# One pipeline over the eight retention and feed-forward units of a hybrid transformer kernel, with its first normalizations in one pass

## What is computed

```python
x = x + retention_net(layernorm(x))    # 2 layers
x = x + experts(layernorm(x))          # 8 experts, top 2 of the router
x = x + causal_attention(layernorm(x)) # 16 heads of 8 channels
x = x + experts(layernorm(x))          # same weights
# retention_net, for each layer:
p = layer_norm(x) @ proj_w + proj_b ; q, k, v, xo = split(p)
ret = ((q @ k.T) * D[head]) @ v        # D: decaying lower triangle, 16 heads
x = x + (ret * silu(xo)) @ reto_w + reto_b
h = layer_norm(x)
x = x + gelu(h @ ffn1_w + ffn1_b) @ ffn2_w + ffn2_b    # 128 -> 512 -> 128
```

## Time and profile before

| | |
|---|---|
| median of 3 runs | 881.59 us (880.51 to 881.97) |
| the profiled execution | 881.72 us |
| its span, first to last instruction | 879.9 us |
| busy: TensorE, DVE, ScalarE, GpSimd | 74%, 71%, 38%, 33% |
| first retention tile on DVE | 38.5 us |
| retention of layer 0, feed-forward 0, retention 1 end at | 121, 168, 252.7 us |
| first scatter of GpSimd, first product of an expert | 301.3, 347.0 us |
| mean granted clock of TensorE | 0.884 of full speed |

### The profile page before, as it was taken

How to read it: one execution, slowest core, us unless ns; L and a number is a source line. 1 busy time by engine, 2 the same in 40 slices (tenths; PEclk the granted TensorE clock), 3 DMA queues, 4 the chain that set the end, 5 groups by cost and what they waited for, 6 DMA issues and landing times.

```text
span 879.9 us, 19404 instructions
## 1 busy us (share of the span) xinstructions
PE 647.0 (74%) x6492; PEld 446.0 (51%) x6492; DVE 628.8 (71%) x1935; ACT 338.0 (38%) x581; POOL 289.8 (33%) x554
## 2 busy tenths in 40 slices
PE   2597888777888311999925788898888972499990
PEld 0254546444556211999923244444444432499990
DVE  6887935787947982888854788677678735388874
ACT  1423143434244311444414055565564561244440
POOL 1223441113464474455522001110512222355551
PEclk9999989999999655999966599999999995699995
DMA  9301189821120011656534421322312000255554
GB/s 208 124 2 50 62 151 181 119 88 39 68 67 1 26 52 51 171 165 168 165 96 127 103 57 30 85 50 56 102 50 52 11 17 16 79 167 160 166 151 149
DMA packets 102627, 81.01 MB, mean 92 GB/s; under 512 B 8381, under 2 KB 92797, under 8 KB 102365
## 3 DMA queue, kind: packets, MB, share of 16 engines
q1 hardware_dynamic: 97744, 70.19, 32.5%
q0 software_dynamic: 4544, 9.38, 3.1%
q10 hardware_dynamic: 240, 0.20, 0.1%
HBM read 54.56 MB, written 23.20 MB: 88 GB/s over the span
## 4 chain that ended last, share of the span: by engine, by line
PE 52%; DVE 21%; issue 9%; POOL 6%; ACT 5%; DMA 5%; SPq 1%; DVEq 0%; ACTq 0%; POOLq 0%
PE PC L1982 8%; PE PA L1972 6%; PE PB L1972 6%; DVE rmax L1327 4%; POOL rows_dram L739 4%; PE P L2063 4%; PE PC L1931 3%; PE PA L2023 3%; PE PA L2021 3%; DVE pm L954 2%; PE PA L1843 2%; PE PA L1920 2%; PE PC L1866 2%; PE PC L2046 2%; PE PB L1920 2%
## 5 line engine op out<-in xcount | busy, mean ns | idle before, releaser
L1327 DVE TENSOR_REDUCE rmax<-PA 128x1 f32<-128x512 f32 (+3 forms) x256 | 120.2, 489 | 49.2 <-PE PA L2023 42.3
L751 POOL DMA_INDIRECT outs_dram<-va,ids x78 | 81.3, 1042 | 93.0 <-DVE va L1266 89.2
L739 POOL DMA_INDIRECT rows_dram<-va,idx x64 | 63.1, 986 | 79.8 <-DVE va L1195 61.1
L1982 PE MATMUL PC<-ffn_w,pm 128*128 128x128 f32 x624 | 86.9, 282 | 1.3 <-DMA ffn_w<-in_w 1.2
L2023 PE MATMUL PA<-kst,qst 96*128 96x512 bf16 (+3 forms) x256 | 83.2, 329 | 0.0
L2021 PE MATMUL PA<-mqb,idb 128*128 128x128 bf16 x256 | 59.9, 235 | 25.4 <-DVE rmax L1327 18.5
L1982 PEld LDWEIGHTS PC<-ffn_w,pm 128*128 128x128 f32 x624 | 75.8, 192 | 2.4 <-DMA ffn_w<-in_w 1.9
L1600 ACT ACTIVATE kv_b<-P 128x256 f16<-128x256 f16 x78 | 29.9, 384 | 112.6 <-PE P L1961 112.6
L1256 DVE SCALAR_TENSOR_TENSOR pm<-PB,invb,decay 128x512 f32<-128x512 f32 x78 | 58.5, 750 | 19.6 <-ACT decay L1608 12.8
L2021 PEld LDWEIGHTS PA<-mqb,idb 128*128 128x128 bf16 x256 | 25.2, 98 | 87.9 <-DVE rmax L1327 48.8
L1972 PE MATMUL PA<-kv_b,pm 128*128 128x128 f16 x936 | 67.6, 224 | 0.0
(11 more groups left out here) (239 smaller groups left out, 1444.4 us busy)
## 6 DMA issues: line engine op xcount, KB each, us to landing
ffn_w<-in_w SPq DMA_DIRECT2D x78, 256.0 KB
rows_dram<-wall SPq DMA_DIRECT2D x1, 8385.0 KB, 51.1
X<-in_w SPq DMA_DIRECT2D x32, 256.0 KB, 2.9
proj_w<-rows_dram SPq DMA_DIRECT2D x78, 65.0 KB, 2.1
qst<-parts_dram SPq DMA_DIRECT2D x48, 96.0 KB
kst<-parts_dram SPq DMA_DIRECT2D x48, 96.0 KB
parts_dram<-qkp SPq DMA_DIRECT2D x16, 256.0 KB, 2.6
X<-in_x SPq DMA_DIRECT2D x8, 256.0 KB, 5.0
```

The lines of the kernel that those rows point to most:

```text
L739: nc.gpsimd.indirect_dma_start(out=rows_dram, out_offset=bass.IndirectOffsetOnAxis(ap=idx[:, t, r:r + 1], axis=0), in_=xrow[:, t, :], in_o ...
L751: nc.gpsimd.indirect_dma_start(out=outs_dram, out_offset=bass.IndirectOffsetOnAxis(ap=ids[:, k % YB:k % YB + 1], axis=0), in_=ysb[:, k % Y ...
L1327: nc.vector.tensor_reduce(rmax[:, i, h % HG:h % HG + 1], PA[:, n % 2, 0:(i + 1) * P], AX_X, ALU.max).then_inc(pair_sb[n % 2], 1)
L1982: ins = mm(PC[:, k % 2, 0:D], eT[:, k % 2, f, :], w2b[k % WB2][:, f, :], start=f == 0, stop=f == FB - 1)
```

## The change

- **Loop.** `retention` and `feed_forward` become one loop `blocks()` over 8 units n (layer, sequence) of 4 tiles: t runs through 32 tiles and two more steps, n, u = divmod(t, 4). The feed-forward of unit n-2 lies in unit n: ffn1's products two and two in u = 0 and 1, ffn2's in u = 3. The turn of unit n+1 stands in u = 2, its query and key products behind the retained tile, and the turn for the feed-forward of unit n-1 at the end of u = 3.
- **Order.** `retain(t-1)`, with the product of the masked scores, stands ahead of the ffn1 products of the step.
- **Buffers.** Feed-forward products go through the ring of two banks, ten uses for a unit; each bank has a semaphore of its own. `hT` moves to the space of `qst`.
- **Normalizations.** `norm_twice` takes the statistics once and computes both inverse roots together (v+e and v(1+e)+e^2), then writes `xn` and `R` from `X`. Sequence 0 is done ahead of the loop, sequences 1, 2 and 3 at the ends of steps 0, 3 and 5. Layer 1's input normalization goes the way of the others: sums on DVE, factors on GpSimd (a step later), rows on ScalarE.
- **Side work.** Largest weights in steps 7 to 14, the scales in step 17, high and low halves one in each of steps 18 to 25. The final normalization of sequence 0 (`leave(0)`) stands in step 30 of DVE.
- **Loads.** The constants, sequence 1 and the decay mask are issued by ScalarE; the fill of `rows_dram` by SyncE ahead of all expert weights.
- **Comparisons.** Two of 256 elements instead of eight of 64 in each choice of the router.

```diff
+            def norm_twice(s):
+                for k in range(TPS):
+                    ins = nc.vector.bn_stats(st6[:, k, :], X[:, TPS * s + k, :])
...
+                nc.vector.tensor_scalar(rs[:, 0, 0:TPS], mv[:, 0:TPS, 1], EPS, None, ALU.add)
+                link(nc.vector.tensor_scalar(rs[:, 0, TPS:2 * TPS], mv[:, 0:TPS, 1], 1.0 + EPS, EPS * EPS,
+                                             ALU.mult, ALU.add))
+                y = inverse_roots(2 * TPS)
+                for out, o in ((xn, TPS), (R, 0)):
+                    for k in range(TPS):
...
+                ins.then_inc(xn_ready, 1)
```

The new loop of TensorE:

```diff
+                for t in range(LAST + 2):
+                    n, u = divmod(t, TPS)
+                    if t < LAST:
+                        keys_values(t)
+                        scores(t)
+                        if u == 0:
+                            gate_input(n)
...
+                    if t >= 2:
+                        project_out(t - 2)
...
+                    if u == 2 and n + 1 < UNITS:
+                        plain_turn(*ln_in(n + 1))
+                    if 1 <= t < LAST + 1:
+                        retain(t - 1)
+                    if u < 2 and n >= 2:
+                        up(n - 2, 2 * u, 2 * u + 2)
+                    if u == 2 and n + 1 < UNITS:
+                        queries_keys(n + 1)
+                    if u == 3 and n >= 2:
+                        down(n - 2)
+                    if u == 3 and n >= 1:
+                        plain_turn(*ln_up(n - 1))
+                route(0, 0)
+                down(UNITS - 2)
+                plain_turn(*ln_up(UNITS - 1))
+                up(UNITS - 1, 0, FB)
+                count(0, 0).then_inc(ring_ps, 1)
+                down(UNITS - 1)
```

Of DVE (the order in a step is: keys and values, state, this `add_ffn`, `decay_q`, mask PA, add out, mask PB, sums, gate, and then what follows here):

```diff
+                    if u == 0 and n >= 3:
+                        add_ffn(n - 3)
+                        if u == 3 and n + 1 < UNITS:
+                            decay_q(n + 1)
...
+                    if u == 0 and 3 <= n < SEQ + 3:
+                        row_sums(R, n - 3)
+                        means(*ln_in(n + 1))
+                    if t in (0, 3, 5):
...
+                        norm_twice(s)
...
+                    if E - 1 <= t < 2 * E - 1:
+                        largest_weight(t - E + 1)
+                    if t == 2 * E + 1:
                         weight_scales()
+                    if 2 * E + 2 <= t < 3 * E + 2:
+                        low_weight(t - 2 * E - 2)
+                    if t == LAST - 2:
+                        leave(0)
```

Of ScalarE (`weights(t)` is `high_weight(t - 18)` for t from 18 to 25, and nothing else):

```diff
+                for n in range(UNITS + 2):
+                    if n < UNITS:
+                        gate_input(n)
...
+                    if n >= 2:
+                        gelu(n - 2, 0)
+                        gelu(n - 2, 1)
+                    weights(TPS * n)
+                    if n >= 2:
+                        gelu(n - 2, 2)
+                        gelu(n - 2, 3)
+                    weights(TPS * n + 1)
+                    if n + 1 < UNITS:
+                        if n + 1 >= SEQ:
+                            normalize(*ln_in(n + 1))
+                        turn_queries_keys(n + 1)
+                    weights(TPS * n + 2)
+                    if n == UNITS:
+                        normalize(LNM1, 0)
+                        logits(0, 0)
+                    if 1 <= n <= UNITS:
+                        normalize(*ln_up(n - 1))
+                        plain_turn(*ln_up(n - 1))
+                    weights(TPS * n + 3)
```

And of DVE on the way out:

```diff
             def leave_and_route():
-                leave(0)
+                mean_factors(STAT[ln_up(UNITS - 1)])
                 leave(1)
                 route(0, 0)
+                add_ffn(UNITS - 2)
                 leave(2)
                 choose_slots(0, 0)
+                add_ffn(UNITS - 1)
                 route(0, 1)
                 choose_slots(0, 1)
                 leave(3)
```

667 lines of the change are left out of this document (297 added, 370 removed).

## The result

The kernel before ran at 881.05 us beside the changed one (median of 4 runs, 880.21 to 881.97), the changed one at 889.97 (4 runs, 886.93 to 892.55). The ratio is 1.0100, with a 95% interval of 1.0065 to 1.0134: the change makes the kernel 1% slower. I had forecast 867.5 and a range up to 884. The profiled execution took 889.34 us, with a span of 887.3.

The account below looks back on a forecast made before the run. TensorE was taken to bound units at 25.3 us, plus waits including 20.9 for weight halves; the first scatter comes 13.4 us earlier and 0.7 is saved later, so span 865.8, predicted time 867.5 us, range 843 to 884.

Parts of the forecast that it names:

- The sum of a unit: In a unit with feed-forward, TensorE's work totals 25.3 us against DVE's 21.2, so TensorE bounds it unless kept waiting.
- some 1 us ... early on: In the first two units, TensorE's lower clock was booked at some 1 us.
- a wait for a load that never came: DVE reaches its first largest weight at 73.5 but waits for that weight's load until 77.
- Start: Up to step 8: first keys at 20.8, first mask 22.1, first largest weight 73.5, step 8 at 76.
- The fill of `rows_dram`: Rival at the start: expert weights landing behind this fill only after 90, not 77, cancel the gain; 882, chance 0.04.
- Units 2 and 3: Steps 8 to 16, the first units with feed-forward, take 50.6 + 1 us.
- The coupling: In steps 18 to 25 low halves wait for ScalarE's high halves, delaying keys and values; TensorE waits 20.9 us.
- no coupling: Rival: the weight halves cost nothing because ScalarE or DVE runs further ahead; 22.3 us more gained, 845, chance 0.22.
- Table loads: Silu and gelu alternating adds 10.2 us of loads, costed at nothing as hidden; rival: on the path, 878, chance 0.1.
- Way out: From step 28 to the first scatter: 61.1 us, retention done at 262.1, first scatter at 287.9.
- a pure gain: At the start, `norm_twice` saves 4 x 3.4 = 13.6 us, largely paid back by uncovered waiting for the first queries.
- TensorE idles at the borders of units as before: Rival: idling of 4.3 us a unit stays in six units, costing 26 us; 893, chance 0.13.

Follow-up runs that it names:

- e14: The changed kernel with the weights' low halves one step later, plus dummy products in TensorE's three long waits of the first two units; 860.35 us.
- e10: The changed kernel with the weights' low halves one step later and each sequence's first two normalizations in two passes again; 877.85 us.
- e4: The changed kernel with silu in place of gelu in the feed-forwards, so ScalarE needs no table change between the two; 889.60 us.
- e9: The changed kernel with the weights' low halves one step later and GpSimd's last three wide additions ahead of its factors for sequence 1; 864.26 us.
- e5: The changed kernel with the weights' low halves one step later and leave(0) at the end of step 31 instead of 30; 865.55 us.
- e8: The kernel before with only each sequence's first two normalizations done in one pass (norm_twice); 880.92 us.
- e1: The changed kernel with DVE writing the weights' low halves one step later, in steps 19 to 26 instead of 18 to 25; 866.01 us.
- e3: The changed kernel with dummy products added in TensorE's four longest waits, in steps 19, 20, 23 and 24; 882.58 us.
- e11: The changed kernel with low halves one step later, sequence 1 normalized ahead of the loop, leave(0) in step 31 and GpSimd's three additions early; 856.76 us.
- e2: The changed kernel with the normalization of sequence 1 ahead of the loop, behind that of sequence 0; 883.09 us.

## Why the prediction was wrong, step by step

The side was wrong, most of the mechanisms were right, and the step that failed is mainly one: **every wait was priced at its length alone, and TensorE's work behind it at its upper clock.** The sum of a unit takes all its terms from rows of work without a gap, and then adds 20.9 us of waits. The clock stood in the text once, as "some 1 us ... early on". The runs showed 11.2 us for it in units 4 to 6, and 4.7 that come back in the first two units when the waits are filled. Beside it, of the 20.3 us by which the first scatter is late, stand waits that were sized too small or left out (2.3 us in units 4 to 6, and two borders at the start) and an interplay of DVE and GpSimd that no step had (3.1). Products put some 3 us too high in all, and a wait for a load that never came, hid part of these.

- **Start.** DVE's first copy (21.5 for 20.8), first mask (23.0 for 22.1) and `norm_twice` (5.65 us for 5.8) were right. TensorE's three idle stretches in the first six steps are 3.2, 4.3 and 5.8 us for "three stretches of 5.8". Step 8 is 4.9 us late, but the sum missed by more: DVE comes to its first largest weight at 81.84 for 73.5. The 3.5 us that the sum had for the load of that weight, and that never came, hid part of it. Filled waits of TensorE give back 4.7 (e14). The border of sequences at the end of the second unit makes DVE wait 2.7 us for keys and queries, for which the sum had nothing, and the one at the end of the first unit 4.2 even in e14, for 2.3. The fill of `rows_dram` took 54.0 us to land, at 75.7, and kept nothing waiting: that rival falls.
- **Units 2 and 3.** 51.2 us for 51.6. TensorE's waits are 1.8 in them (for 1 in the sum), and its products were put some 0.6 us a unit too high.
- **The coupling.** Place, cause and order were right, and the copies and products that stand behind it. TensorE's waits over tiles 16 to 28 are 25.6 us for 23.3 in the sum. Its products take 84.9 for 75.9; at a clock of 1.00 they would take 73.7 (e10), so the lower clock costs 11.2 us, and a sum that was 2.2 too high hid part of that. Taking the coupling away gives 24.8 us, not 20.9. The rival "no coupling" falls.
- **Table loads.** Hidden, as costed (e4). That the prediction's 889 for them at a higher price lies at the measured time is chance.
- **Way out.** 65.6 us for 61.1. 3.1 of the 4.5 are DVE's three short operations beside GpSimd's wide ones, which no step had, and removing them gave 2.3 (e9). The other 1.4 are in the chain from step 30 to the end of the retention (25.3 for 23.9), behind the 6.75 us wait that `leave(0)` makes (retained tile 1.94 again); e5 moved that wait and did not remove it, so that the clock is the reason there is argued, not shown.
- **What DVE gains at the start.** The text calls 4 x 3.4 us "a pure gain" of `norm_twice`. It is 12 us in the new layout (e10), and none that can be measured in the old (e8): the row of DVE that I rested on the earlier trace rows hid a wait of TensorE for loads until 29.1, and I had not read that wait in TensorE's own timeline.
- **The rival that came true in its side.** "TensorE idles at the borders of units as before" was to decide from 2.3 us a unit on. In units 2 and 3 TensorE waits 1.5 us once at a border; with the coupling gone there is a border wait of 2.4 us in two of the units 4 to 6, but behind a GpSimd chain and not through PA, PB and PC. Its 893 was near the time and its reason was not the reason.

From the first scatter to the end the profiled executions take 578.1 to 583.2 us, and the quicker versions no less than the others (579.1 in the changed kernel and in e5, 581.3 in e1). The lists there are the same, so a difference of a few us between two single traces says nothing by itself.

## What to carry to other kernels

Price a wait of TensorE at its length plus what the products behind it may lose at the lower clock: look up in the trace one group of products at either level (here 1.08 and 1.94 us) and count how many follow. Make a range of it for short waits, since the same one left the clock up in one execution and not in the next. Where two engines make the halves of one thing in the same step, put the second half one step later before doing anything else; that one line was worth 24 us here. And before a shorter operation is booked as a gain, read the timeline of the other engines beside it for a wait that ends at the same time.

## What the runs showed of the hardware that I had not expected

- Dummy products in a wait make a program shorter: some 11 us (46 products in three places) gave 5.7 us (e14), and 52 products in four places 7.4 (e3). Part of both is the luck of the clock elsewhere: unit 3 took 26.5 us in the profiled execution of e14 and 28.0 in that of e1_low_late.
- The same wait leaves the clock up or not. Behind 1.48 us at the turn of unit 3 the retained tile takes 1.08 us in the changed kernel, e10, e11 and e14, and 1.94 in e1, e2, e3, e4, e5 and e9; over the next 3.6 us the granted clock is 1.00 in the changed kernel, over the next 3.9 us 0.56 in e1. With the same 7.6 us of waits in units 4 to 6, TensorE was busy for 78.0 us in e1 and 73.7 in e10.
- DVE's operations on 4 columns last 1.19 us in place of 0.16 beside a GpSimd addition of 1.27 us on 512 columns, and end with it. The Trainium skill (SBUF — State Buffer, SBUF: two separate sides) says that the two engines share a pair of ports as an exclusive lock, held for a whole instruction, and that a DVE operation with two inputs from SBUF meets it; the rows agree.
- The same gain of DVE time was worth 12 us in one layout and nothing measurable in another (e10, e8).
